# A graph layer on one core: layer norm by groups, h's low halves in quarter pieces, and x minus (1+gate) h formed in the last pass

## What is computed

```python
h = jnp.maximum(_layernorm(x, axis=-1), 0.0)
deg = jnp.clip(adj.sum(axis=1), 1.0)
dis = deg ** (-0.5)
diffusion = (dis[:, None] * adj * dis[None, :]) @ h - h
norms = jnp.maximum(jnp.linalg.norm(h, axis=-1), COS_EPS)
sim = h @ h.T / (norms[:, None] * norms[None, :])
attn = jax.nn.softmax(beta * sim * adj, axis=1)
out = x + diffusion + jax.nn.sigmoid(alpha) * (attn @ h - h)
```

## Time and profile before

| | |
|---|---|
| median of three runs | 1989.08 us |
| lowest, highest | 1988.24, 1989.92 us |
| the profiled execution | 1987.21 us |
| its span by the profile | 1985.4 us |
| prologue, to the first cosine matmul | 145.5 us |
| first loop, to the last matmul of the sums | about 1363 us |
| turn-over, to the first matmul of the last pass | 17 us |
| last pass and output | about 460 us |

### The profile page before, as it was taken

One profiled execution on the slowest core, in us unless ns is written; L12 is line 12 of the kernel. 1 busy time (PEld: TensorE's weight loads), 2 busy tenths in 40 slices (PEclk: granted clock), 3 DMA queues, 4 the chain that ended last, 5 costly groups with the idle time before them and its releaser, 6 DMA issues.

```text
span 1985.4 us, 44628 instructions
## 1 busy us (share of the span) xinstructions
PE 1823.4 (92%) x19602; PEld 1408.8 (71%) x19602; DVE 1238.0 (62%) x1347; ACT 1304.8 (66%) x1259; POOL 1309.4 (66%) x788
## 2 busy tenths in 40 slices
PE   0029999999999999999999999999996999999997
PEld 0026777777777777777777777777775888888887
DVE  4677778778777877887887787787775201111110
ACT  3639989898988989988998898899886000000000
POOL 2568998999999899999999999999882000000000
PEclk9989999999999999999999999999998999999999
DMA  9347887678887678887688886788316645454520
GB/s 168 65 129 98 101 108 99 92 98 104 101 108 98 97 95 106 101 107 97 97 96 107 100 106 97 97 98 106 76 51 237 237 167 188 153 191 153 188 96 12
DMA packets 179671, 229.38 MB, mean 116 GB/s; under 512 B 8340, under 2 KB 155796, under 8 KB 174228
## 3 DMA queue, kind: packets, MB, share of 16 engines
q0 software_dynamic: 135168, 67.13, 43.7%
q1 hardware_dynamic: 26644, 151.01, 20.5%
q10 hardware_dynamic: 17664, 8.39, 1.6%
HBM read 348.13 MB, written 79.69 MB: 215 GB/s over the span
## 4 chain that ended last, share of the span: by engine, by line
PE 85%; POOL 5%; DVE 4%; ACT 3%; issue 2%; DMA 1%; SPq 0%; ACTq 0%; POOLq 0%; DVEq 0%
PE cos_ps L610 30%; PE cos_ps L669 11%; PE top_ps L669 11%; PE top_ps L640 11%; PE top_ps L644 11%; PE top_ps L642 10%; POOL ustage L286 5%; ACT arena L311 1%; ACT xe L329 1%; DMA asb<-x_in 1%; DVE vc L412 1%; DVE ssq L451 1%; SPq L207 0%; ACT xe L318 0%; DVE ssq L450 0%
## 5 line engine op out<-in xcount | busy, mean ns | idle before, releaser
L286 POOL TENSOR_TENSOR ustage<-xe,ustage 128x1024 f16<-128x1024 f32 x512 | 1094.7, 2142 | 128.0 <-ACT xe L364 122.6
L526 DVE TENSOR_TENSOR xe<-cos_ps,arena 128x1024 f32<-128x1024 f32 x512 | 626.9, 1225 | 280.9 <-PE cos_ps L610 181.5
L360 ACT ACTIVATE ustage<-xe,ebias,ab 128x1024 f16<-128x1024 f32 x512 | 635.4, 1241 | 133.0 <-DVE xe L526 131.6
L640 PE MATMUL top_ps<-h,ustage 128*128 128x129 f16 x4096 | 719.3, 221 | 2.9 <-POOL ustage L286 2.9
L644 PE MATMUL top_ps<-h,ustage 128*128 128x129 f16 x4096 | 719.2, 220 | 0.0
L642 PE MATMUL top_ps<-hlo,ustage 128*128 128x128 f16 x4096 | 718.5, 219 | 0.0
L364 ACT ACTIVATE xe<-xe,ebias,ab 128x1024 f32<-128x1024 f32 x512 | 628.2, 1227 | 0.0
L640 PEld LDWEIGHTS top_ps<-h,ustage 128*128 128x128 f16 x4096 | 400.2, 98 | 65.9 <-POOL ustage L286 3.5
L642 PEld LDWEIGHTS top_ps<-hlo,ustage 128*128 128x128 f16 x4096 | 400.1, 98 | 59.1
L644 PEld LDWEIGHTS top_ps<-h,ustage 128*128 128x128 f16 x4096 | 400.2, 98 | 0.0
L501 DVE TENSOR_REDUCE top_ps<-arena 128x8 f32<-128x1024 uint16 x256 | 311.7, 1218 | 0.0
(11 more groups left out here) (90 smaller groups left out, 1144.7 us busy)
## 6 DMA issues: line engine op xcount, KB each, us to landing
arena<-adj_in_dram POOLq DMA_DIRECT2D x256, 256.0 KB, 8.8
at_scratch<-arena SPq DMA_DIRECT2D x128, 512.0 KB, 3.8
arena<-at_scratch SPq DMA_DIRECT2D x26, 2048.0 KB, 8.0
xe<-at_scratch SPq DMA_DIRECT2D x6, 2048.0 KB, 7.9
asb<-x_in SPq DMA_DIRECT2D x16, 256.0 KB, 10.5
h_scratch<-arena SPq DMA_DIRECT2D x4, 1024.0 KB, 5.6
base_scratch<-asb SPq DMA_DIRECT2D x4, 1024.0 KB, 5.0
arena<-h_scratch SPq DMA_DIRECT2D x1, 4096.0 KB, 13.5
```

The lines of the kernel that those rows point to most:

```text
L286: nc.gpsimd.tensor_tensor(elo[:, n % ES, :], ef[:, n % XS, :], ehi[:, n % ES, :], ALU.subtract).then_inc(elo_done, 1)
L360: nc.scalar.activation(ehi[:, n % ES, :], xm[:, n % XS, :], ACT.Exp, bias=ebias[:, 0:1], scale=ab[:, 1:2]).then_inc(ehi_done, 1)
L526: nc.vector.tensor_tensor(xm[:, n % XS, :], cos_ps[:, n % 2, :], at8[:, m % W, :, n % B], ALU.mult).then_inc(x_done, 1)
L640: nc.tensor.matmul(top_ps[:, bank, col:col + P + 1], head, h1[:, s, 0:P + 1], start=(first and t % 3 == 0), stop=final, skip_group_check=True)
```

## The change

It has five parts.

1. **x first, from two queues.** SP issues x's DMAs for q = 0, 1 and ACT those for q = 2, 3 at the head of its list. POOL waits for all of x before it issues the 16 DMAs of adj chunks 0 and 1.
2. **Layer norm by groups.** DVE's `ln(g)` takes statistics, root and correction for 16 tiles; ACT's list is written anew, with relu and unit_rows in halves of 8 tiles and the roots between the halves. DVE's list is ln(0), ln(1), square_sums(0), norms(0), ln(2), square_sums(1), norms(1), split(0), ln(3), copy_uT(0), square_sums(2), norms(2), split(1), copy_uT(1), square_sums(3), split(2), norms(3), copy_uT(2), split(3).
3. **h's tail in pieces.** `hlo` is made in 16 pieces of four tiles. Eight stand before the first loop, eight in it, after rest(n) for n = 2 to 9. PE waits for a piece every four units of the first panel. The loads of chunk 2 go from before the loop to n = 11 to 18, those of chunk 3 from n = 13 to 20 to n = 19 to 26; later ones stay. DVE's first transpose waits for tiles 0 to 31 of h alone (h_kept[0], h_kept[1]) and 8 pieces.
4. **No base in the prologue.** L271, L275 and the four stores L215 go, with base_scratch and the waits on them.
5. **Base in the last pass.** load_base loads, for each half of a panel, h (one DMA, to `hp`, which lies where y32 was) and x itself (four DMAs, to `o2`): 10 DMAs for each panel instead of 2. load_base(0) and (1) stand behind dis * h and wait for all of y. DVE makes x - (1+gate) h with one instruction of 128 x 1024 at the head of each panel.

```diff
-            for g in range(CH):
-                sp.wait_ge(base_ready, g + 1)
-                sp.dma_start(base_dram[:, g * GW:(g + 1) * GW],
-                             x_st[:, 16 * g:16 * (g + 1), :].rearrange("p s d -> p (s d)")).then_inc(base_kept, 16)
...
+            for g in range(CH):
+                pool.wait_ge(x_loaded[g], 16 * Q)
+            for k in range(2):
+                for part in range(8):
+                    load_rows(k, part)
+
+            def tail_of_h(four):
+                tiles = slice(4 * four, 4 * (four + 1))
+                pool.wait_ge(hhi_ready, four // 4 + 1)
                 nc.gpsimd.tensor_tensor(hlo[:, tiles, :], h32[:, tiles, :], h1[:, tiles, 0:P], ALU.subtract).then_inc(hlo_ready, 1)
-                nc.gpsimd.tensor_scalar(ptmp[:, :], h32[:, tiles, :].rearrange("p s d -> p (s d)"),
-                                        neg_1_gate[:, 0:1], None, ALU.mult).then_inc(scaled, 1)
-                nc.gpsimd.tensor_tensor(xg, xg, ptmp[:, :], ALU.add).then_inc(base_ready, 1)
...
             for n in range(UNITS):
                 rest(n)
+                if 2 <= n < 10:
+                    tail_of_h(n + 6)
+                for k in range(2, CHUNKS):
+                    part = n - first_unit(k)
+                    if 0 <= part < 8:
...
+                        load_rows(k, part)
...
-            load_base(0)
-            load_base(1)
             act.wait_ge(h_back, 16)
             act.wait_ge(dis_ready, 1)
...
+            act.wait_ge(y_ready, PANELS)
+            load_base(0)
+            load_base(1)
...
+            def ln(g):
+                of = slice(16 * g, 16 * (g + 1))
+                dve.wait_ge(x_loaded[g], 16 * Q)
+                for s in range(16 * g, 16 * (g + 1)):
+                    last = nc.vector.bn_stats(out=stats[:, s, :], in_=x_st[:, s, :])
+                link(last)
...
-            dve.wait_ge(h_kept, 16 * CH)
-            dve.wait_ge(hlo_ready, CH)
-            dve.wait_ge(base_ready, CH)
+            dve.wait_ge(h_kept[0], 16)
+            dve.wait_ge(h_kept[1], 16)
+            dve.wait_ge(hlo_ready, 8)
             turn(0)
...
-                dve.wait_ge(base_loaded[panel % 2], 16 * 2 * (panel // 2 + 1))
+                dve.wait_ge(base_loaded[panel % 2], 16 * 10 * (panel // 2 + 1))
+                link(nc.vector.scalar_tensor_tensor(out=o, in0=hp[:, panel % 2, :, :], scalar=neg_1_gate[:, 0:1], in1=o,
+                                                    op0=ALU.mult, op1=ALU.add))
```

More of the change, by code:

```diff
@@ L138, in gnn_block_kernel @@
         SL = len(slots)
+        hp = ustage[:, 0:2 * PW].rearrange("p (k t d) -> p k t d", k=2, d=P)
         o2 = ptmp[:, :].rearrange("p (k t d) -> p k t d", k=2, d=P)
@@ L165, in gnn_block_kernel @@
         hlo_ready = sem("hlo_ready")
[L166 to L169, removed]
+        h_kept = [sem(f"h_kept{g}") for g in range(CH)]
         rows_loaded = [sem(f"rows_loaded{s}") for s in range(RS)]
@@ L307, in _, with var_root @@
[L307 to L314, removed]
+            def var_root(g):
+                of = slice(16 * g, 16 * (g + 1))
+                act.wait_ge(var_ready, g + 1)
+                nc.scalar.activation(vb[:, of], va[:, of], ACT.Sqrt).then_inc(std_ready, 1)
@@ L315, in relu, with square @@
+            def relu(g, half):
+                if half == 0:
+                    act.wait_ge(ln_ready, g + 1)
+                for s in range(16 * g + 8 * half, 16 * g + 8 * (half + 1)):
+                    nc.scalar.activation(h32[:, s, :], x_st[:, s, :], ACT.Relu, scale=rstd[:, s:s + 1],
+                                         bias=shift[:, s:s + 1]).then_inc(relu_done, 1)
+            def square(g):
+                act.wait_ge(relu_done, 16 * (g + 1))
                 if g >= 1:
@@ L318, in relu, with ssq_root @@
                 nc.scalar.activation(sq, hg.rearrange("p s d -> p (s d)"), ACT.Square).then_inc(sq_ready, 1)
-            def unit_rows(g):
+            def ssq_root(g):
+                of = slice(16 * g, 16 * (g + 1))
                 act.wait_ge(ssq_ready, g + 1)
[L322 to L340, removed]
+                nc.scalar.activation(vb[:, of], ssq[:, of], ACT.Sqrt).then_inc(norm_root, 1)
+            def head_of_h(g):
+                nc.scalar.activation(h1[:, 16 * g:16 * (g + 1), 0:P], h32[:, 16 * g:16 * (g + 1), :], ACT.Copy).then_inc(hhi_ready, 1)
+            def unit_rows(g, half):
+                if half == 0:
+                    act.wait_ge(rnorm_ready, g + 1)
+                    if g >= 1:
+                        act.wait_ge(u_split, g)
+                for s in range(8 * half, 8 * (half + 1)):
+                    last = nc.scalar.activation(u32t[:, s * P:(s + 1) * P], h32[:, 16 * g + s, :], ACT.Copy,
+                                                scale=rnorm[:, 16 * g + s:16 * g + s + 1])
+                if half == 1:
+                    last.then_inc(u_ready, 1)
@@ new lines, in _ @@
+            var_root(0)
+            relu(0, 0)
+            var_root(1)
+            relu(0, 1)
+            square(0)
+            relu(1, 0)
+            ssq_root(0)
+            relu(1, 1)
+            square(1)
+            head_of_h(0)
+            unit_rows(0, 0)
+            var_root(2)
+            unit_rows(0, 1)
+            relu(2, 0)
+            ssq_root(1)
+            relu(2, 1)
+            square(2)
+            head_of_h(1)
+            unit_rows(1, 0)
+            var_root(3)
@@ L342, in copy_acc @@
+            unit_rows(1, 1)
+            relu(3, 0)
+            ssq_root(2)
+            relu(3, 1)
+            square(3)
+            head_of_h(2)
+            unit_rows(2, 0)
+            unit_rows(2, 1)
+            ssq_root(3)
+            head_of_h(3)
+            unit_rows(3, 0)
+            unit_rows(3, 1)
             def copy_acc(panel):
```

110 lines of the change are left out of this document (52 added, 58 removed).

## The result

The changed kernel takes 1930.31 us (median of four, 1929.91 to 1930.59) against 1989.17 (median of four, 1988.24 to 1989.92), a ratio of 0.9704, 95% interval 0.9687 to 0.9721. The forecast was 1930. The profiled execution's span is 1928.3 us; before it was 1985.4.

| | before | after | gain | forecast |
|---|---|---|---|---|
| first Relu | 37.4 | 15.2 | 22.2 | at 13.5 |
| end of the last unit row | 137.2 | 81.7 | 55.5 | at 81 |
| first cosine matmul | 145.5 | 90.2 | 55.3 | a gain of 56 |
| last sums of the loop | 1508.8 | 1459.5 | 49.3 | a gain of 50 (6 lost in the loop) |
| first matmul of the last pass | 1525.8 | 1468.8 | 57.0 | a gain of 57.7 |

What follows compares the result with a forecast made beforehand. PE was taken to bound the loop and last pass, leaving prologue and turn-over to gain: 56 - 6 + 7.7 = 57.7 us off 1987.2 gives 1929.5, taken as 1930; range 1919 to 1945.

Steps and rivals of the forecast that it cites:

- The bound: Whole kernel: PE bounds the first loop and last pass, so only the prologue and the 17.1 us turn-over can gain.
- The prologue, 56: Start to first cosine matmul: it comes at 89.3 instead of 145.5, a gain of 56 us, between 50 and 60.
- The layout: Prologue: row durations put end to end in the new order, with waits; ACT ends at 83, taken as 81.
- The loop, 6 lost: First loop: tail pieces and chunk loads make POOL the bound of the first 27 units, costing 6 us.
- The turn-over, 7.7: Between loop and last pass: ACT's base loads no longer hold up dis * h, a gain of 7.7 us.
- The last pass, nothing: Last pass: extra DMAs and the added DVE instruction fit in idle time; no change, 1 to 2 us per panel if uncovered.
- A: Turn-over: it gives nothing, as h may come back only at 1521; 1938 us, chance 0.12.
- C: First loop: the tail pieces cost it nothing, at 0.98 us each; 1924 us, chance 0.06.
- D: Last pass: small loads of x and h slow adj's chunks and the kernel gets slower, 2042 at 18 us landing; chance 0.02.
- E: Loop start: an older wait, such as the adj chunks, holds it, for instance at 110; 1951 us, chance 0.04.
- B: Prologue: it gives less, from slow issues on ACT (+5) and small steps held up by pieces (+5); 1940 us, chance 0.14.
- The signs: Trace times: first Relu 12 to 15, last unit row 79 to 84, first cosines 87 to 92, loop waits 4 to 7 us.

Runs made afterwards that it cites:

- b_base_last: The kernel before with no base in the prologue, base made in the last pass and its loads behind dis * h; 1962.85 us, ratio 0.9871.
- b_no_pool: b_base_last without the four tails on POOL, h's low half set to zero at the start; 1946.45 us, ratio 0.9790.
- a_tails_early: The changed kernel with all 16 tail pieces before the loop, the last four after the last norms, chunks 2 and 3 loaded as before; 1926.08 us.
- a_adj_first: The changed kernel with POOL's first 16 loads of adj issued at once, beside x, without waiting for x; 1929.09 us, ratio 0.9702.
- a_warm_both: a_tails_early with 36 unneeded matmuls in the turn-over and 12 and 4 behind the third and fourth groups' transposes; 1923.31 us, ratio 0.9672.
- b_turnover: The kernel before with one edit: load_base(0) and load_base(1) stand behind dis * h on ACT; 1980.52 us, ratio 0.9959.
- b_ln_groups: The kernel before with layer norm by groups alone, ln(0) to ln(3) in a row at the head of DVE's list; 1977.84 us, ratio 0.9952.
- a_one_queue: The changed kernel with all 16 DMAs of x issued from SP, adj still waiting for x; 1928.93 us, ratio 0.9699.

## Why the prediction was right, step by step

**The bound.** PE was busy in the loop and the last pass: 1290.0 of 1290.0 us, from the copy of the first panel to the last sums 1186.0 us in both kernels, and in the last pass 459.5 us against 459.6. Right.

**The prologue, 56.** 55.3 measured. The layout's parts: first Relu at 13.5 was 1.7 us too early, as x's first group landed at 8.93 and not at 7.3, and each ln(g) took 6.3; ACT's waits after it came to 6.6 us (8.6 laid out), of them 2.5 for the last norms (2.7). So the waits were 2.0 us shorter than laid out; the instructions overlapped by 0.9, where 2 had been taken off. ACT ended 0.7 late, the first cosines came 0.9 late. The small steps beside the pieces lost 2.6 us (3 laid out). That it was POOL's work which held up the norms is shown by b_base_last and b_no_pool.

**The loop, 6 lost.** 6.0 measured, but only half of it for the stated reason, and this is the term that was mis-sized. Pieces and loads cost 3.1 (a_tails_early). A piece in the loop takes up 1.04 us, not 1.24 (rest follows rest after 3.17), so the excess was 8 x 0.52 = 4.2 and not 5.8. And POOL's lead was larger than 1.8: its third rest ends at 104.78 (98.12 + 6.66), 2.5 us before PE's third sums, where in the kernel before it is 0.8 at the same unit:

```profile
98.12 6.66 POOL L275 TENSOR_TENSOR ustage<-xe,ustage 128x1024 f16<-128x1024 f32 x3 [43.39 <-ACT xe L398]
```

```profile
107.26 0.22 PE L686 MATMUL top_ps<-h,ustage 128*128 128x129 f16 x1
```

In a_adj_first, where PE began at full rate, the lead is 2.4 and the loss by pieces and loads 3.1 as well. So the slow first units did not make the lead; the dip, which holds PE back just there while POOL goes on, fits.

The rest is PE's clock: 1.3 us in the first units, which a_warm_both gets back, and 1.6 us for the dip, from which the profile of before was free. Its first panel took 177.3 us from the first cosines, those of b_turnover, b_base_last and b_ln_groups, with the same work in the loop, 178.9; the copies that end them, of before and of b_turnover (first cosines at 145.48 and 145.28):

```profile
322.76 1.16 ACT L346 ACTIVATE asb<-top_ps 128x387 f32<-128x387 f32 x3 [0.37 <-PE top_ps L644]
```

```profile
324.21 1.16 ACT L346 ACTIVATE asb<-top_ps 128x387 f32<-128x387 f32 x3 [0.37 <-PE top_ps L644]
```

The prediction had nothing on the clock. Two errors of 3 us cancelled, and that part of the agreement is luck.

**The turn-over, 7.7.** 7.7 measured, from 17.05 to 9.35 us, in the whole and in b_turnover alone.

**The last pass, nothing.** Right, but the cover was thinner than it looked. Panel 0's ten loads took 15.9 us to issue, as much as the slow case that was laid out (16), four of them 12.4, beside four chunk loads of SP's; then they took another 11 to land, so that its base was complete only at 1512.4. With 3.5 us of DVE work behind it, 11 us were left before the matmuls ended. Later panels wait 48 us.

**The rivals.** A fell in b_turnover, C in that the pieces do cost the loop 3 us, D in the length of the last pass, and E in that DVE's first transpose follows split(3) at once, at 85.2. B's stalls were there but small (2.6 us beside the pieces; ACT's eight issues of x took 3.8 us, not 1.2 each).

**The signs.** Two of them came out outside their range: the first Relu at 15.2 (12 to 15), and the loop's loss to POOL, put at 4 to 7 us of waiting and measured as 3.1. The last unit row, the first cosines, the small steps (1.04 at most), dis * h (0.1 us behind dis) and the panels (55.89, the first 58.0 as before) lie where they were put.

**The scale.** The forecast was made from a profiled execution of 1987.2, 1.9 us below the median, and the result of the sum, 1929.5, was then moved to 1930 for the median. Between the two profiled executions the gain is 57.1, between the medians 58.9. The dip of 1.6 us that only the profile of before lacks would account for the difference if its other executions had it; they have no trace, so this is not shown. b_turnover, whose profile has the dip, points the same way: 6.5 us less by spans, 7.7 by medians.

## What to carry to other kernels

An engine that nobody waits for can still set the pace: lay its timeline beside the small instructions of the chain, and where the same instruction takes 0.17 us once and 3.6 us another time, look for what ran beside it on POOL or DVE. An edit's worth belongs to the schedule around it: x first was worth 8 us alone, and in the finished kernel either half of it could be undone at no cost. And test a sum that comes out right term by term; here one term came out right only because PE's clock took what POOL did not.

## What the runs showed of the hardware

- POOL and DVE block each other both ways: a small step of DVE is held until POOL's piece ends (0.17 to 1.04 us beside pieces, to 3.6 beside whole tails), and four pieces of POOL take 5.54 instead of 4.35 us beside such steps.
- PE ran its first four pairs of cosine matmuls at half rate in most of the new kernels and in b_no_pool, behind 5.9 us of idleness, 3.6 us of transposes and 1.3 us of idleness. The record of after has a granted clock of 1.00 there, that of a_one_queue 0.50, at the same matmul durations: durations tell the clock more finely than the record. The rate was full in a_adj_first after the same pattern, and in the kernel before and in its variants that keep the tails, where the idleness ahead of the transposes was 9.5 to 14.3 us; what decides between the two is open.
- With 36 further matmuls in the turn-over the first panel of the last pass took 56.05 us instead of 57.83. With 16 further matmuls in the prologue the first sums came 1.3 us sooner behind the first cosines, in one profile.
- While SP had four chunk loads of 2 MB under way, ACT needed 12.4 us to issue four DMAs of 64 KB. The next four took 7.3 us, and otherwise four take 2.1 to 3.1. That it is SP's loads which hold them up was not tested.
